# Attention over edges: tiles of 128 edges gathered once into a ring, their rows copied from there piece by piece

## The reference

```
h = (x @ W_att).reshape(n, H, D); a_src, a_dst = head logits of h
e = a_src[src] + a_dst[dst];  e = where(e > 0, e, 0.2 * e)
m = segment_max(e, dst);  e = exp(e - m[dst]);  s = segment_sum(e, dst)
out = segment_sum((e / s[dst])[:, :, None] * h[src], dst)   # then mean over heads, bias, two-layer MLP, norms
```

## Time and profile before

| | us |
|---|---|
| median of 3 runs | 8874.27 |
| lowest to highest | 8874.23 to 8877.43 |
| profiled execution | 8873.14 |
| its span, first to last instruction | 8871.4 |
| GpSimd busy in the span | 6291.7 (71%) |
| VectorE busy | 5689.4 (64%) |
| TensorE matmul busy | 4987.9 (56%) |
| ScalarE busy | 2440.1 (28%) |
| gathers of line 1918, 2016 of them, busy | 1991.8 |

### The profile page before, as it was taken

How to read it: one execution, slowest core, us unless ns; L and a number is a source line. 1 busy time by engine, 2 the same in 40 slices (tenths; PEclk the granted TensorE clock), 3 DMA queues, 4 the chain that set the end, 5 groups by cost and what they waited for, 6 DMA issues and landing times. The chain is left out here.

```text
span 8871.4 us, 111269 instructions
## 1 busy us (share of the span) xinstructions
PE 4987.9 (56%) x30696; PEld 3836.2 (43%) x30696; DVE 5689.4 (64%) x16260; ACT 2440.1 (28%) x4235; POOL 6291.7 (71%) x5733
## 2 busy tenths in 40 slices
PE   5888888888679999356666666666673000000000
PEld 3445454454458777345555555555572000000000
DVE  6888888888689999366666666666683222222222
ACT  0111111111045555035555555555531000000000
POOL 4888888888845555367777777777725777777776
PEclk8888888888779999555555555555555555555555
DMA  3333333333411111123333333333331222222221
GB/s 85 35 35 35 35 35 35 35 35 35 55 43 23 22 23 23 34 53 57 56 57 57 56 57 56 57 56 57 55 88 48 53 53 50 53 53 53 53 49 48
DMA packets 637857, 421.33 MB, mean 47 GB/s; under 512 B 533495, under 2 KB 545684, under 8 KB 635712
## 3 DMA queue, kind: packets, MB, share of 16 engines
q0 software_dynamic: 322560, 216.89, 20.6%
q1 hardware_dynamic: 312926, 197.07, 7.7%
q10 hardware_dynamic: 2304, 6.55, 0.2%
HBM read 234.91 MB, written 185.18 MB: 47 GB/s over the span
## 5 line engine op out<-in xcount | busy, mean ns | idle before, releaser
L1918 POOL DMA_INDIRECT rows_l<-att_row_table,slots_l x2016 | 1991.8, 988 | 647.7 <-issue 614.1
L890 POOL DMA_INDIRECT acc<-val,idx x1240 | 1918.8, 1547 | 417.8 <-issue 372.2
L1140 POOL DMA_INDIRECT rows_l<-relation_table,idx x1612 | 1533.0, 951 | 509.2 <-issue 491.0
L1153 DVE SCALAR_TENSOR_TENSOR run<-run,mask,rows_l 128x64 f32<-128x64 f32 x1612 | 459.6, 285 | 1568.9 <-DMA rows_l<-relation_table,idx 1513.3
L699 PE MATMUL banks<-part 128*128 128x490 bf16 (+1 forms) x5580 | 1297.4, 392 | 0.0
L1189 PE MATMUL banks<-run,link 128*128 128x64 f32 x98 | 21.1, 422 | 2043.7 <-PEq L1120 2043.7
L2039 PE MATMUL banks<-rows_l,prob 128*128 128x65 f32 x4032 | 919.0, 420 | 44.4 <-ACT piece_part L1973 41.0
L2039 PEld LDWEIGHTS banks<-rows_l,prob 128*128 128x128 f32 x4032 | 877.9, 331 | 105.5 <-issue 86.3
L1189 PEld LDWEIGHTS banks<-run,link 128*128 128x128 f32 x98 | 21.0, 333 | 2044.4 <-issue 2044.4
L1291 POOL DMA_INDIRECT gathered_rows<-h_table,gathered_index x600 | 577.7, 963 | 446.9 <-ACT gathered_index L1401 273.5
L699 PEld LDWEIGHTS banks<-part 128*128 128x128 bf16 x5580 | 584.2, 107 | 638.1 <-issue 153.7
(11 more groups left out here) (402 smaller groups left out, 10401.2 us busy)
## 6 DMA issues: line engine op xcount, KB each, us to landing
piece_sums<-kept_l SPq DMA_DIRECT2D x252, 264.0 KB
running_sums<-run SPq DMA_DIRECT2D x62, 832.0 KB, 3.5
attr<-in_edge_attr SPq DMA_DIRECT2D x61, 624.0 KB, 3.9
rows_l<-att_row_table,slots_l POOLq DMA_INDIRECT x2016
rows_l<-relation_table,idx POOLq DMA_INDIRECT x1612, 2.4
acc<-val,idx POOLq DMA_INDIRECT x1240, 3.2
gathered_rows<-h_table,gathered_index POOLq DMA_INDIRECT x600
acc<-zero ACTq DMA_DIRECT2D x12, 512.0 KB, 16.2
```

The lines of the kernel that those rows point to most:

```text
L890: e.indirect_dma_start(acc_d[k], bass.IndirectOffsetOnAxis(ap=idx[h][:, r:r + 1], axis=0), val[h][:, r, :], None, compute_op=ALU.add).then ...
L1140: e.indirect_dma_start(gbuf[h][:, r, :], None, table, bass.IndirectOffsetOnAxis(ap=idx[h][:, r:r + 1], axis=0))\
L1153: e.scalar_tensor_tensor(run[h][:, r, :], before_row, mask[h][:, r:r + 1], row, ALU.mult, ALU.add).then_inc(s_step, 1)
L1918: e.indirect_dma_start(rows[u][:, r, :], None, hx_d, bass.IndirectOffsetOnAxis(ap=slots[u][:, r:r + 1], axis=0))\
```

## The change

A piece no longer begins at its block's first edge. The edge list is cut into its 1612 fixed tiles of 128, and a piece is now the pair of a tile and a block that it meets, so that a tile that several blocks share gives as many pieces; edges of other blocks in it are masked as before by the node digits. Their number is at most 1612 + 392, and the count of units stays 252.

- GpSimd gathers each tile once, in 202 groups of up to eight (201 full ones and one of four), written out without a loop, into `gathered`, a ring of TRING = 8 groups. From the ninth group on it first loads a number of units from `gate` into a register and waits until ScalarE has copied the tags of so many. At the start of group g it waits for the landing of group g - 2 and then counts it in `s_there`.
- SP, in each turn, loads the number of groups needed (`need`) into a register, waits for it on `s_there` and for the rows buffer to be free, and then eight times loads a position from `place` and copies 128 rows of 308 bytes from there in the ring to `rows[u]` (SBUF to SBUF). Then it stores the kept sums of six units back. Before the store was all it did.
- ScalarE no longer copies `slots`.
- The preparation counts only blocks (16 counting operations instead of 32), makes `place`, `need` and `gate`, stores them to DRAM word by word and loads them back as rows of one partition; sources are loaded by tile with 13 plain DMAs from SP instead of 16 gathers on GpSimd.
- Some buffers share memory: exponentials and fade factors lie in the `run` buffers, windows of sources and logits in `block_logits` and `block_rows`. The first layer's last part counts tiles and no longer counts pieces of its own.

The diff, cut to what acts on the time:

```diff
@@ preparation, SP
+                    for w in range(TW):
+                        e.dma_start(src_w[0:tiles_in(w), w, :],
+                                    srcp_d[w * P * P:(w * P + tiles_in(w)) * P].rearrange("(t p) -> t p", p=P))\
+                         .then_inc(s_srcw, 16)
...
+                    e.wait_ge(s_place, 2)
+                    with nc.allow_non_contiguous_dma(reason="from a column for each piece to one row"):
+                        e.dma_start(place_d.rearrange("n (w p) -> p n w", p=P), where_i[:, :, :]).then_inc(s_where, 16)
+                        e.dma_start(gate_d.rearrange("(w p) -> p w", p=P), gate_i[:, :]).then_inc(s_where, 16)
...
+                    e.wait_ge(s_where, 32)
+                    e.wait_ge(s_wt, TW)
+                    e.dma_start(place[:, :], place_d[0:1, 0:NQ * QUAD]).then_inc(s_where, 16)
...
+                        e.dma_start(need[:, :], place_d[1:2, 0:NQ * QUAD].rearrange("n (j r) -> n j r", r=QUAD)[:, :, QUAD - 1])\
+                         .then_inc(s_where, 16)
+                    e.dma_start(gate[:, :], gate_d.unsqueeze(0)).then_inc(s_where, 16)
@@ preparation, GpSimd
-                        e.indirect_dma_start(src_w[:, w, :], None, srcp_d.rearrange("(a b) -> a b", b=P),
-                                             bass.IndirectOffsetOnAxis(ap=start_i[:, w:w + 1], axis=1)).then_inc(s_win[w // 4], 16)
@@ preparation, VectorE
-                        e.scalar_tensor_tensor(junk[2 * (w % 2) + 1][:, :], thru[:, :], kidx[:, w:w + 1], pads[:, :],
-                                               ALU.is_le, ALU.mult, accum_out=skip[:, w:w + 1]).then_inc(s_cnt, 1)
...
+                    e.tensor_scalar(where_i[:, 0, :], tile_i[:, :], TRING * QUAD - 1, None, ALU.bitwise_and).then_inc(s_cnt, 1)
+                    e.tensor_scalar(where_i[:, 1, :], tile_i[:, :], 3, None, ALU.logical_shift_right).then_inc(s_cnt, 1)
...
@@ loop, GpSimd
-                    with e.Fori(0, ROUNDS) as i:
-                        for u in range(RING):
-                            j = i * RING + u
-                            e.wait_ge(s_slot, j + 1)
-                            e.wait_ge(s_sum, j + 1)
-                            e.sem_inc(s_pace, 1)
-                            for r in range(QUAD):
-                                e.indirect_dma_start(rows[u][:, r, :], None, hx_d,
-                                                     bass.IndirectOffsetOnAxis(ap=slots[u][:, r:r + 1], axis=0))\
-                                 .then_inc(s_got[u], 16)
+                    def landed(g):
+                        e.wait_ge(s_tile[g % TSEMS], 16 * sum(tiles_of(m) for m in range(g % TSEMS, g + 1, TSEMS)))
+                        e.sem_inc(s_there, 1)
+
+                    for g in range(TU):
+                        if g >= TRING:
+                            units = nc.values_load(gate[0:1, g:g + 1], [mybir.EngineType.Pool], min_val=1, max_val=NQ,
+                                                   skip_runtime_bounds_check_because=SMALL_SUM)
+                            e.wait_ge(s_as, units)
+                        if g > 1:
+                            landed(g - 2)
+                        for r in range(tiles_of(g)):
+                            t = g * QUAD + r
+                            e.indirect_dma_start(gathered[:, g % TRING, r, :], None, hx_d,
+                                                 bass.IndirectOffsetOnAxis(ap=src_col[:, t:t + 1], axis=0))\
+                             .then_inc(s_tile[g % TSEMS], 16)
+                    landed(TU - 2)
+                    landed(TU - 1)
@@ loop, ScalarE
-                        e.copy(slots[u][:, :], slot_src[:, bass.ds(j * QUAD, QUAD)]).then_inc(s_slot, 1)
@@ loop, SP
+                    def load(i, u):
+                        j = i * RING + u
+                        units = nc.values_load(need[0:1, bass.ds(j, 1)], [mybir.EngineType.SP], min_val=1, max_val=TU,
+                                               skip_runtime_bounds_check_because=SMALL_SUM)
+                        e.wait_ge(s_sum, j + 1)
+                        e.wait_ge(s_there, units)
+                        for r in range(QUAD):
+                            col = nc.values_load(place[0:1, bass.ds(j * QUAD + r, 1)], [mybir.EngineType.SP], min_val=0,
+                                                 max_val=(TRING * QUAD - 1) * ROW,
+                                                 skip_runtime_bounds_check_because=SMALL_SUM)
+                            e.dma_start(rows[u][:, r, :], flat[:, bass.ds(col, ROW)]).then_inc(s_got[u], 16)
...
+                    def turn(i, u):
+                        if real(*at(i, u, 1)):
+                            load(*at(i, u, 1))
+                        if real(*at(i, u, -6)):
+                            store(*at(i, u, -6))
+                    load(0, 0)
+                    sweep(e, turn, 6)
```

More of the change, by code:

```diff
@@ L1599, in build @@
             spare = [t[:, :, :].rearrange("p r f -> p (r f)") for t in run]
-            ones, thru, pads = (spare[0][:, k * NB:(k + 1) * NB] for k in range(3))
+            ones, thru, tilerow = (spare[0][:, k * NB:(k + 1) * NB] for k in range(3))
             junk = [spare[1][:, k * NB:(k + 1) * NB] for k in range(4)]
@@ new lines, in _ @@
+                    e.wait_ge(s_cnt, KW + 9)
+                    e.sem_inc(s_place, 1)
+                    for w in range(NG2):
+                        e.scalar_tensor_tensor(junk[w][:, :], tilerow[:, :], gidx[:, w:w + 1], ones[:, :],
+                                               ALU.is_le, ALU.mult, accum_out=gcnt[:, w:w + 1]).then_inc(s_gate, 1)
+                    e.wait_ge(s_gate, NG2)
+                    e.scalar_tensor_tensor(gcnt[:, :], gcnt[:, :], float(QUAD), gidx[:, :], ALU.add, ALU.add)\
+                     .then_inc(s_gate, 1)
@@ L1866, in build @@
             rows = [sb(f"rows_l2_{u}", [P, QUAD, ROW], f32, ctx) for u in range(RING)]
-            slots = [sb(f"slots_l2_{u}", [P, QUAD], i32, ctx) for u in range(RING)]
+            gathered = sb("tile_rows", [P, TRING, QUAD, ROW], f32, ctx)
             kept = [sb(f"kept_l2_{u}", [P, QUAD, KEPT], f32, ctx) for u in range(RING)]
@@ L1871, in build @@
             lin = [sb(f"edge_logit_{u}", [P, QUAD, P], f32, ctx) for u in range(2)]
-            exp = [sb(f"edge_exp_{u}", [P, QUAD, P], f32, ctx) for u in range(2)]
+            spare = [t[:, :, :].rearrange("p r f -> p (r f)") for t in run]
+            exp = [t[:, 0:QUAD * P].rearrange("p (r a) -> p r a", a=P) for t in spare]
             prob = [sb(f"prob_{u}", [P, QUAD, P], f32, ctx) for u in range(2)]
-            fade = [sb(f"fade_{u}", [P, W1, 1 + QUAD], f32, ctx) for u in range(2)]
+            fade = [t[:, QUAD * P:QUAD * P + W1 * (1 + QUAD)].rearrange("p (f r) -> p f r", r=1 + QUAD) for t in spare]
             part = [sb(f"piece_part_{u}", [P, W1, 1 + QUAD], f32, ctx) for u in range(2)]
@@ L1906, in sweep, with tiles_of @@
                     turn(ROUNDS, u)
+            def tiles_of(g):
+                return min(QUAD, T - g * QUAD)
+            SMALL_SUM = "clamped from below where it is made, and the blocks and tiles that it counts are given by the shapes"
             with nc.Block() as block:
```

165 lines of the change are left out of this document (98 added, 67 removed).

## The result

| | before | after |
|---|---|---|
| median, us | 8874.6 (4 runs, 8874.23 to 8877.43) | 8760.1 (4 runs, 8756.73 to 8762.98) |
| profiled execution, its span | 8873.14, 8871.4 | 8756.73, 8755.0 |
| ratio | | 0.987 (0.9853 to 0.9887) |

The kernel is faster, by 114.5 us where 430 were forecast. The time lies in the wide range (8395 to 9240), but outside the forecast's own (8395 to 8520), and what sets it is not what I forecast: SP is the bound, as in the first rival, with a turn of 9.9 us.

What follows compares the result with a forecast made beforehand. POOL's gather issue was taken as the bound: loop and drain from 2646 to 2221 us (2151 + 70), -425, preparation -6, together -431, so 8445 us; own range 8395 to 8520 (chance 0.52), wide range 8395 to 9240.

Steps and rivals of the forecast that it cites:

- the first rival: SP's queue in the loop becomes the bound, kernel still faster: 9.5 us a turn, 8693 us; chance 0.23.
- POOL's side: GpSimd's loop time: 1612 gathers at 1.248 us, plus stretches and gate loads, 2151 us or 8.54 a turn.
- gate loads: GpSimd's register load and wait from the ninth group on: 194 of them, 49 us in all.
- stretches: Lengthening of GpSimd's gathers in the loop, taken to come from the consumers' turn: 90 us over 252 turns, unchanged.
- the DMA engines: Transfers in the loop: 68 to 85 of 137 engine-us a turn, half to 0.6, not a bound.
- the word stores: Two stores of single words in the preparation: 5 us, ending before the logits' store, so hidden.
- preparation: Attention layer's part ahead of the loop: fewer counting operations on DVE move its chain by -6 us.
- the drain: From GpSimd's last gather issued to the next stage: 70 us, where it was 40 before.
- X: Cost on SP and POOL of one register load from SBUF: estimated 0.2 us; SP no longer hidden from 0.47.
- SP's turn is then 6.1 us: SP's queue per loop turn, 4.3 us plus nine register loads; claimed hidden under POOL's 8.54.
- the 0.14 for waits and loop: Allowance in SP's turn for four waits and the loop: 0.14 us.
- ACT's wait for rows: ScalarE's wait in each loop turn for rows to arrive: down from 3.1 to about 1 us.

Runs made afterwards that it cites:

- e1: The changed kernel with one register load for a unit's eight positions in place of eight loads; 8440.0 us, ratio 0.9531 to the kernel before.
- e7: The changed kernel with seven DMAs a turn: four copies from the ring, two same-size reads from the DRAM row table, one of twice that; 8441.1 us.
- e5: The changed kernel with the store of the kept sums issued from ScalarE's queue in place of SP's; 8540.3 us, ratio 0.9635 to the kernel before.
- e12: The kernel of e8 (two register loads of four positions), run four times as base for scan variants; 8452.0 us, ratio 0.9518 to the kernel before.
- e2: The changed kernel with four copies and four position loads a turn in place of eight, other rows constant; 8488.4 us.
- e6: The changed kernel with one register load for eight positions and the store on ScalarE's queue; 8503.2 us, ratio 0.9596 to the kernel before.
- e4: The changed kernel without position loads: four single and two double copies a turn from fixed places; 8490.9 us.
- e8: The changed kernel with two register loads of four positions each per turn; 8424.5 us, 0.9505 of the median before.
- e11: The kernel of e12 with the scan's factors a constant 0.5 in PSUM, fading left out; 8297.0 us.

## Why the prediction was right and where it failed

**Right.** POOL's side held as a sum: 1612 gathers at 0.944 + 0.30, no wait for the ring while POOL is the bound, 2157 us against 2151, and a ratio of 0.9531 in e1, 8458 us at the time before of 8874.6, against the forecast 8445. That it is so close is luck in part: gate loads 49 us too high and stretches 55 us too low cancel. It is the time of a kernel whose SP keeps up, and this one does not. Right were also that the DMA engines are not the bound, that the word stores stay off the path (preparation -7.7, forecast -6), and the drain, as long as POOL is the bound (65 in e1, forecast 70). X was estimated at 0.2 and measured 0.267.

**The step that failed** is "SP's turn is then 6.1 us, under POOL's 8.54 with 2.4 to spare". It takes 9.9. The 3.8 us that were missing, term by term:
- "a DMA with a register position and 128 rows costs SP 0.332 (that of the running sums)": a copy with both sides in SBUF costs 0.486 (e7). 8 x 0.154 = 1.2 us.
- Instructions were summed by their durations, and the gap of some 0.04 us between two of them had no term but the 0.14 for waits and loop. 8 x 0.16 = 1.3 us, of which 0.3 was covered by address arithmetic that I priced too high: 1.0.
- X itself: 9 x 0.067 = 0.6 us.
- The turn's beginning and the store: 1.9 us beside the eight copies, where need load, store and allowance made 0.8 + 0.1 for the load's excess: 1.0. Some 0.5 of it is the one long load of the turn (0.785 for 0.267), the rest gaps and wait instructions; e5 shows 0.83 for the store where I had 0.45.

1.2 + 1.0 + 0.6 + 1.0 = 3.8. None would have been decisive alone. I had named one unknown, X, and given it all of the uncertainty; with the true price of the rest (9.9 - 9 x 0.267 = 7.5 in place of 4.3) SP would have ceased to be hidden from X = 0.12, not 0.47.

**The outcome is the first rival's, on other grounds.** It had SP at 9.5 us a turn and 8693; SP at 9.9 gave 8760. Where the forecast's 425 us in loop and drain went: 104 came. Had SP kept up, 8447 to 8458 would stand there (the ratios of e12 and e1), so about 300 us were turned into a new wait, POOL's 287 us at the ring gate, and into a longer drain (133 in place of 65), since SP was further behind when POOL ended. The part of the forecast that said ACT's wait for rows would fall to 1 us a turn failed with it: 712 us, 2.8 a turn (1.5 in e1, where SP keeps up).

**What I took for granted and was half right about**: "the stretches come from what the consumers do in a turn". They come from one operation, the scan, once a turn, but their size is no constant: 89 us before, 116 after, 145 in e1, 150 in e12, 200 in e2 and e6. A difference of 50 us between variants can be this phase alone.

Open is why copies issued back to back start no less than about 0.64 us apart (e1, e4), and by what way the store of the kept sums holds up a register load on SP's queue some 1.6 us later.

## What to carry to other kernels

A queue's engine that issues many small DMAs is an engine like the others: sum its turn with every instruction, with the gap behind each, and with the DMA price of the same pair of memories, and give the sum's uncertainty to all terms, not to the one that has no row. After the run, look for the engine that has no wait at all. Positions should be loaded several at a time, and where GpSimd's gathers are the bound, a long DVE operation with two SBUF inputs is worth cutting into pieces (tried here with the scan alone) or giving one input in PSUM.

## What the runs showed of the hardware

- Issuing a DMA from SP cost 0.486 us for SBUF to SBUF and 0.334 for DRAM to SBUF, at the same shape and with a register position in both; twice the bytes cost the same (e4, e7).
- Copies SBUF to SBUF with no register load between them started 0.64 us apart, with register positions (e1) and without (e4).
- A load into a register from SBUF took SP 0.267 us for one word (after), 0.299 for four (e8, the second of a turn) and 0.527 for eight (e6), on GpSimd 0.289 for one, there hidden beside the running gather.
- A load under way some 1.6 us after a store of 264 KB was issued took about 0.5 us longer (0.785, 0.747 and 1.03 for one, four and eight words), and in e5, where ACT issued the store, one load of SP's turn was as long.
- A scan with both inputs in SBUF holds a gather's descriptor work until its end; with one input in PSUM it does not (mean gather 1.037 against 0.944, e12 and e11). A multiplication of two SBUF inputs holds it as well (2.73 us for a gather in the kernel before). The Trainium skill ("SBUF — State Buffer", section "Who interferes with whom") says that a DVE operation with two SBUF inputs contends with a GpSimd instruction that reads SBUF, and with this the runs agree. It infers that `tensor_tensor` does not stall the making of descriptors, and here it did, for up to its own length.
